# The first gelu of a pipelined FFN step, and its gate, moved behind the square, the key copies and the norms of the same slot

## The reference

```python
for i in range(6):
    x = attn_layer(shift_tokens(x), Wqkv[i], q_scale[i], k_scale[i], Wo[i]) + x
    x = ffn_layer(shift_tokens(x), ln_g[i], ln_b[i], W1[i], b1[i], W2[i], b2[i]) + x
```

## Time and profile before

| what | value |
|---|---|
| median of 3 runs | 2605.0 us (2604.25 to 2606.4) |
| the profiled execution | 2607.1 us, span 2605.3 us |
| PE busy | 2383.1 us (91%) |
| DVE busy | 1763.3 us (68%) |
| ACT busy | 1625.6 us (62%) |
| POOL busy | 1605.3 us (62%) |
| mean granted TensorE clock | 0.967 |

### The profile page before, as it was taken

The page is one execution under the profiler, slowest core; times in us unless marked ns, Lnnn a source line. Parts: engine busy times, 40 slices in busy tenths (PEclk is TensorE's granted clock), DMA queues, the critical chain, the costliest instruction groups (busy, mean ns, idle before and its releaser), DMA issues.

```text
span 2605.3 us, 57541 instructions
## 1 busy us (share of the span) xinstructions
PE 2383.1 (91%) x22655; PEld 1632.9 (63%) x22655; DVE 1763.3 (68%) x2708; ACT 1625.6 (62%) x3162; POOL 1605.3 (62%) x931
## 2 busy tenths in 40 slices
PE   5769999999999999999999999999997888889998
PEld 3436666666666666666666666666665666656665
DVE  2348777777777777777777777777774888852332
ACT  1127777777777777777777777777773666643332
POOL 1039878887888788878887888788872222301111
PEclk8879999999999999999999999999997999989999
DMA  4002223222232222322233222322223000000000
GB/s 107 0 21 59 53 55 75 69 63 55 59 79 69 55 59 62 78 63 59 53 78 71 59 54 54 87 66 54 54 56 102 1 1 1 1 1 5 5 2 8
DMA packets 77196, 127.11 MB, mean 49 GB/s; under 512 B 24948, under 2 KB 48770, under 8 KB 76930
## 3 DMA queue, kind: packets, MB, share of 16 engines
q1 hardware_dynamic: 76930, 123.42, 20.3%
HBM read 26.56 MB, written 1.07 MB: 11 GB/s over the span
## 4 chain that ended last, share of the span: by engine, by line
PE 45%; DVE 26%; issue 13%; ACT 12%; POOL 4%; DMA 0%; SPq 0%; ACTq 0%; POOLq 0%; DVEq 0%
DVE qk L1211 7%; PE bank L604 7%; PE bank L527 5%; PE bank L563 5%; PE bank L813 4%; PE obank L584 4%; DVE n L1218 4%; PE bank L618 3%; ACT qk L900 3%; DVE bank L1235 3%; PE obank L823 2%; PE bank L823 2%; DVE sh L1227 2%; DVE mx L1223 2%; DVE mx L1365 2%
## 5 line engine op out<-in xcount | busy, mean ns | idle before, releaser
L1211 DVE TENSOR_TENSOR qk<-bank,tab 128x1024 f32<-128x1024 f32 x384 | 468.7, 1221 | 308.4 <-ACT qk L900 308.4
L1519 POOL TENSOR_TENSOR qk<-qk 128x1024 f32<-128x1024 f32 x192 | 454.6, 2368 | 284.0 <-DVE qk L1211 284.0
L1523 POOL TENSOR_TENSOR rn<-n2m,cst 128x16 f32<-128x16 f32 x192 | 562.6, 2930 | 16.0
L527 PE MATMUL bank<-wqk,xs 128*128 128x512 f32 x768 | 404.4, 609 | 46.0 <-ACT kT L926 43.0
L1527 POOL TENSOR_TENSOR qk<-qk,rn 128x1024 f32<-128x1024 f32 x192 | 365.2, 1902 | 28.2 <-POOL rn L1523 0.9
L900 ACT ACTIVATE qk<-bank 128x512 f32<-128x512 f32 x384 | 227.1, 591 | 213.8 <-PE bank L527 208.4
L538 PEld LDWEIGHTS bank<-cst,qk 128*128 128x128 f32 x1536 | 192.3, 141 | 210.5 <-issue 186.4
L1531 POOL TENSOR_TENSOR lnr<-lnv,cst 128x2 f32<-128x2 f32 (+1 forms) x88 | 66.3, 753 | 382.4 <-DVE lnv L1105 382.4
L538 PE MATMUL bank<-cst,qk 128*128 128x128 f32 x1536 | 231.7, 274 | 7.5 <-POOL qk L1527 7.5
L1218 DVE TENSOR_REDUCE n<-qk 128x16 f32<-128x1024 f32 x192 | 232.1, 1209 | 0.0
L912 ACT COPY vp<-lnbank 64x512 f32<-64x512 f32 x384 | 225.0, 586 | 9.4
(11 more groups left out here) (195 smaller groups left out, 4387.8 us busy)
## 6 DMA issues: line engine op xcount, KB each, us to landing
vp<-vp SPq DMA_DIRECT2D x672, 130.0 KB, 2.4
wqk<-in_L_ffn_Wqkv SPq DMA_DIRECT2D x24, 256.0 KB, 3.1
wv<-in_L_ffn_Wqkv SPq DMA_DIRECT2D x6, 512.0 KB, 3.6
wo<-in_L_ffn_Wo SPq DMA_DIRECT2D x6, 512.0 KB, 4.2
xs<-Z SPq DMA_DIRECT2D x48, 64.0 KB, 2.0
xs<-Z SPq DMA_DIRECT2D x48, 63.8 KB, 2.0
kT<-rel_by_distance SPq DMA_DIRECT2D x1, 2048.0 KB, 8.1
vp<-in_L_ffn_w SPq DMA_DIRECT2D x1, 2048.0 KB, 13.2
```

The costliest lines, as they stand in the source:

```text
L527: nc.tensor.matmul(bank[s % 2][:, :], xs[:, odd, WIN + r * P:WIN + r * P + P], wqk[:, lo:lo + 512], start=True, stop=True).then_inc(p_full, 1)
L1211: tt(qk[:, both, :].rearrange("p o (h d) -> p o h d", d=DH), heads(bank[c % 2][:, :]).unsqueeze(1).broadcast_to([P, 2, PAIRS, DH]), table. ...
L1519: tt(direct, direct, swapped, ALU.add).then_inc(sum_done, 1)
L1523: tt(rn[:, m % 2, :], n2m[:, :], const("mhalf"), ALU.pow).then_inc(rn_done, 1)
```

## The change

In slot 5 ScalarE runs gelu(f, 0) after the square and the two key copies, instead of first; it still comes ahead of `take_out(i, 2)`. In slot 5 VectorE runs gate(f, 0) after `norms(t, 2)`, instead of between `parts(t, 5)` and the norms; it still comes ahead of the seed. The other two gelus and gates keep their places, and so do all lists of TensorE, GpSimd and SyncE.

```diff
@@ ScalarE, step
                 for s in range(8):
-                    if s in (5, 7) and p2:
-                        gelu(f, s - 5)
+                    if s == 7 and p2:
+                        gelu(f, 2)
                     if s == 7 and p0:
                         exps(t, 0)
...
                     if s < LAG and p1:
                         take_turned(i, s + 8 - LAG, s)
-                    if s == 6 and p2:
-                        gelu(f, 1)
+                    if s in (5, 6) and p2:
+                        gelu(f, s - 5)
@@ VectorE, step
                     if p0:
                         parts(t, s)
-                    if s in (5, 6) and p2:
-                        gate(f, s - 5)
+                    if s == 6 and p2:
+                        gate(f, 1)
...
                     if s % 2 == 1 and p0:
                         norms(t, s // 2)
+                    if s == 5 and p2:
+                        gate(f, 0)
                     if s in (1, 3, 5) and p1:
                         seed(i, s // 2 + 1)
```

## The result

The changed kernel takes 2572.24 us (median; 2571.62 to 2575.51), the one before 2605.07 beside it: the ratio is 0.9875, interval 0.9862 to 0.9888. The forecast was 2570.5. Of the profiled execution the forecast span was 2570.8 us, the measured one is 2570.4.

The account below looks back on a forecast made before the run. TensorE bounds the step loop, idling 1.2 us a step, 0.91 of it waiting for the second key copy; 46 steps x 0.75 us = 34.5 us, taking the median from 2605.0 to 2570.5 us, range 2561 to 2583.

Parts of the forecast that it names:

- ScalarE's sum: ScalarE, slot 5: reordering costs and wins nothing in sum; square and keys come 1.66 us earlier, L945 stays.
- step 48: Step without squares or keys, already in the new order: L945 follows the gelu by 0.37 us, L618 follows L945 by 0.63.
- TensorE's sum: TensorE, slot 6: projection gains 1.0 us, but L618 then waits for L945, so scores come 0.75 us earlier per step.
- The gate as guard of the seed: VectorE: moved gate waits 0.45 us for the gelu; the seed behind it still ends 0.5 us ahead of the scores.
- the cover: VectorE: parts(5) 1.65 us earlier covers the gate's idle half microsecond; without it each further 0.1 us of gelu delays the scores.
- Rival 1: TensorE: all of the idle time comes back, 0.91 to 1.0 us a step, 2559 to 2563 us; chance 8%.
- Rival 2: Part of the gain is lost to a wait hidden today, 0.2 to 0.5 us a step, 2582 to 2596; chance 10%.
- Rival 3: ScalarE's load stays before the square, or only idle time moves: within 5 us of 2605; chance 3%.
- Rival 4: ScalarE: late square or key inputs, no longer covered by load and gelu, make it slower, up to 2647 us; chance 3%.
- Rival 5: ScalarE: after copies out of matmul banks the switch costs a second 1.28 us between load and gelu, 2629 us; chance 1%.

Follow-up runs that it names:

- gelu_alone: Against the kernel before, only ScalarE's gelu(f, 0) moved behind the key copies, VectorE's gate(f, 0) left between parts and norms; 2608.68 us, ratio 1.0015.
- out_first: Against the changed kernel, take_out(i, 2) moved in front of gelu(f, 0), gate(f, 0) left ahead of the seed; 2603.44 us, ratio 0.9993 to the kernel before.
- both: Against the changed kernel, take_out(i, 2) in front of gelu(f, 0) and gate(f, 0) behind the seed; 2550.85 us, ratio 0.9785 to the kernel before.

## Why the prediction was right

- **ScalarE's sum.** The square was to start 0.03 after the exponential, the keys to end at 1.67, the load to start at 1.69, the gelu at 2.99 and L945 at 3.36, counted from that exponential's end. Measured: 0.03, 1.68, 1.70, 2.99, 3.36. L945 didn't move, as step 48 had foretold.
- **TensorE's sum.** L618 was placed at 3.99 and the scores at 5.05; they came at 4.00 and 5.06. 46 x 0.75 = 34.5 us was the sum, 34.4 the stretch's own difference, and the profiled spans differ by 34.9, so only 0.5 lies outside the steps. The medians differ by 32.8. The runs of one kernel spread over 2 to 4 us (2571.62 to 2575.51 for the changed one), and the missing 1.7 us is within that; no run shows where it lies.
- **The gate as guard of the seed.** The seed was placed at 4.55 at its end, and measured at 4.58. The prediction called the 0.5 us up to the scores the cover; 0.15 of it goes from the seed's end to their start, as gelu_alone and out_first show, so a gelu later by more than 0.33 us already comes out in the scores (0.97 came out as 0.64). That without the gate's move nothing would be left of the gain is shown by the half alone (2608.68).
- **Rival 1**, all of the idle time back, fell by L618's 0.24 us of wait, and out_first and both show that this wait can be taken away, but only together with the seed's.
- **Rival 2** fell: the scores came 0.74 earlier and the step is 0.75 shorter, so nothing was lost to a hidden wait behind them. **Rival 3** fell: the load stands right before the gelu.
- **Rival 4** did not happen, but it was a true danger: with keys late by 1.11 us the changed kernel is slower than the old one under the same exchange by 18 us (2623.34 against 2605.68), and the old one doesn't notice. The prediction's own reckoning, that lateness beyond 0.75 us is a loss, gives (1.11 - 0.75) x 46 = 17 us.
- **Rival 5.** The load starts 0.02 us after the second key copy's end and the gelu 0.01 after the load's end, with copies out of the matmul banks straight before it. No further stretch stands there. One of the two arguments against this rival was none: the exponential of step 48 that has copies ahead of it shows no table load of its own, so it says nothing of a switch. What the Trainium skill says of a drain of 1380 ns with every switch (ScalarE: Activation LUTs, "What ACT_TABLE_LOAD costs") is not seen as a gap around the loads here; its 1283 ns for the load is what these traces show.
- **Sizes that were off.** L1211's wait for the square was to fall by 75 us and fell by 61: in slot 6 a new wait of 0.38 us appeared, since the parts there have no backlog in front of them now. The second gelu came 0.6 us earlier, not 0.4. Neither is on the path. The gate's waits for the gelu rose from 7.9 us to 30.7, by 23 where 20 was forecast.

## What to carry to other kernels

Before an operation is moved on an in-order engine, write down for each instruction that it passes who waits for it, and for each that stays behind it how much slack it has: here the sum on ScalarE was zero. The gain came from a waited-for copy that ended 1.65 us earlier, which let TensorE start 1.08 earlier, and it was cut to 0.75 by a second copy that stayed where it was once its 0.84 us of slack was used up. A late producer must take its consumer with it in the other engines' queues, or the consumer blocks what stands behind it; and two edits of which one is harmful and one worthless alone can be worth 21 us together, when the first removes one wait and makes another, and the second removes that one. A table load in front of instructions also hides lateness of their inputs, 1.1 us of it here at no cost, and that cover is lost when the load moves (51 us for the same lateness).

## What was not expected of the hardware

ScalarE's instructions in slot 6 show slightly longer when they follow each other without a gap: the gelu 0.52 us against 0.47, the copy L922 0.61 against 0.58. The copy starts 0.49 us behind the square all the same (1202.89 to 1203.38), as before (0.50, 1222.99 to 1223.49), and nothing here tells where the length comes from. The time outside the 46 steps (the span less the stretch from step 2 to step 48) was 892.5 us in the profile before and 892.0 in the changed kernel's, but 889.9 in both's (2544.9 less 1654.98) and 898.1 in out_first's, with the same instructions there. The profiled execution of both was 4.1 us below its kernel's median and that of out_first 4.4 above, so in these two the spread from run to run lay mostly outside the steps. The length of a step, the same to some 0.02 us from step 5 on but for one or two steps, was the better measure of these edits.
